# Mask products of windowed attention on two strips of 32 rows, with a fixed mask per tile whose outer strip GpSimd copies

## The reference

```
heads = 16, width of a head = 8, W = 32
for each block of 32 queries: keys are the 96 positions from 32 before the block to 32 behind it
scores = q @ k.T                                  (q = k = v = x, no projection)
valid  = |k_pos - q_pos| <= 32 and 0 <= k_pos < 1024
p      = softmax(where(valid, scores, -1e9))
out    = p @ v
x      = layernorm(x + attention block(x)) ...
```

## Time and profile before

| what | us |
|---|---|
| median of 3 runs | 635.5 |
| lowest and highest run | 632.0, 638.23 |
| the profiled execution | 636.62 |
| its span, first to last instruction | 634.8 |
| mean granted TensorE clock | 0.963 of full speed |

### The profile page before, as it was taken

How to read it: one execution, slowest core, us unless ns; L and a number is a source line. 1 busy time by engine, 2 the same in 40 slices (tenths; PEclk the granted TensorE clock), 3 DMA queues, 4 the chain that set the end, 5 groups by cost and what they waited for, 6 DMA issues and landing times.

```text
span 634.8 us, 42631 instructions
## 1 busy us (share of the span) xinstructions
PE 520.3 (82%) x17985; PEld 442.4 (70%) x17985; DVE 530.2 (84%) x1761; ACT 427.5 (67%) x845; POOL 405.0 (64%) x522
## 2 busy tenths in 40 slices
PE   0279999999998989996656879889888888888886
PEld 0167888888887658775545768778777777777775
DVE  5657888898988387876578879999999999999982
ACT  3336776777776457765144768787788878887882
POOL 8434546555652153644227768888888888888882
PEclk9989999999999999998786989999999999999999
DMA  6875984745427010000003232333233322333231
GB/s 203 260 236 175 273 251 149 240 134 196 142 95 253 18 33 18 22 13 2 10 8 76 46 78 53 81 79 79 58 74 79 83 62 66 79 83 69 59 79 45
DMA packets 45201, 64.39 MB, mean 101 GB/s; under 512 B 5488, under 2 KB 37360, under 8 KB 42608
## 3 DMA queue, kind: packets, MB, share of 16 engines
q1 hardware_dynamic: 45168, 63.97, 36.1%
HBM read 36.29 MB, written 8.65 MB: 71 GB/s over the span
## 4 chain that ended last, share of the span: by engine, by line
PE 38%; DVE 36%; issue 12%; DMA 5%; POOL 4%; SPq 2%; ACT 2%; DVEq 1%; POOLq 0%; ACTq 0%
PE ps L756 7%; DVE top L1398 7%; DVE wq_sb L1429 6%; DVE hid L1446 5%; PE ps L815 5%; DVE prod L1455 5%; PE ps L828 4%; DVE r_x L1440 4%; PE ps L736 4%; PE ps L771 4%; DVE best L1409 3%; PE ps L921 3%; PE ps L746 3%; DMA xT<-terms 2%; PE ps L782 2%
## 5 line engine op out<-in xcount | busy, mean ns | idle before, releaser
L921 PE MATMUL ps<-arena,hid 128*32 128x32 f32 x8192 | 80.0, 200 | 43.2 <-DVE hid L1446 35.8
L921 PEld LDWEIGHTS ps<-arena,hid 128*32 128x32 f32 x8192 | 76.1, 112 | 49.4 <-issue 26.0
L970 ACT ACTIVATE arena<-ps 128x512 f32<-128x512 f32 x128 | 70.0, 595 | 55.4 <-PE ps L756 55.2
L1189 DVE TENSOR_REDUCE row_max<-ps 128x8 f32<-128x768 f32 x64 | 61.0, 953 | 19.7 <-PE ps L746 19.3
L930 PEld LDWEIGHTS ps<-xT,downT_sb 128*128 128x128 f32 x528 | 67.1, 199 | 13.1 <-issue 12.0
L756 PE MATMUL ps<-ident,arena 128*128 128x128 f32 x512 | 70.3, 283 | 0.0
L930 PE MATMUL ps<-xT,downT_sb 128*128 (+1 forms) x528 | 66.9, 282 | 0.0
L942 PE MATMUL ps<-up_sb,prod 128*128 128x128 f32 x512 | 65.6, 282 | 0.3 <-DVE prod L1455 0.3
L670 POOL TENSOR_TENSOR wq_sb<-wq_sb,tile_rows 128x1024 f32<-128x1024 f32 x32 | 65.1, 2036 | 0.7 <-POOL tile_rows L664 0.6
L1192 DVE TENSOR_TENSOR arena<-ps,row_max 128x768 f32<-128x768 f32 x64 | 61.3, 958 | 5.1 <-DVE row_max L1189 0.2
L736 PE MATMUL ps<-tile_rows 100*32 100x96 bf16 x2112 | 36.7, 214 | 34.2 <-POOL tile_rows L561 24.9
(11 more groups left out here) (162 smaller groups left out, 1325.9 us busy)
## 6 DMA issues: line engine op xcount, KB each, us to landing
arena<-r_x SPq DMA_DIRECT2D x128, 128.0 KB, 2.4
early<-terms SPq DMA_DIRECT2D x8, 720.0 KB
xT<-terms SPq DMA_DIRECT2D x8, 720.0 KB
hid<-terms SPq DMA_DIRECT2D x8, 720.0 KB
prod<-terms SPq DMA_DIRECT2D x8, 720.0 KB
x_pair<-in_x_wrapped SPq DMA_DIRECT2D x16, 256.0 KB
xT_tile<-xT SPq DMA_DIRECT2D x34, 64.0 KB, 1.9
x<-in_x SPq DMA_DIRECT2D x8, 256.0 KB, 2.7
```

The costliest lines, as they stand in the source:

```text
L921: mm = nc.tensor.matmul(slots[32 * g:32 * g + 32, k, c], leftT[p][:, r // 2, r % 2, :], blocks_of[p][:, :, r // 2, r % 2, GROUP * g:GROUP ...
L970: return nc.scalar.activation(out_ap, in_ap, ACT.Copy)
L1189: V.tensor_reduce(mx.rearrange("p (a b) -> p a b", a=2), sc, AX_X, ALU.max).then_inc(max_done, 1)
```

## The change

The identity of 128 x 128 is replaced by `lanes`: 64 rows in bf16, each strip of 32 rows being four 32 x 32 identities side by side. The mask is the same in each strip of 32 rows, so 32 rows of `lanes` with 32 rows of the mask give the same 128 rows of output. The first group of a half uses rows 0 to 31, the second rows 32 to 63.

The moving operand has a fixed place now: windows 8 to 11 for the first tile of a pair, 12 to 15 for the second. Only one strip of these is not always the same: the first third of window 8 (the first tile may begin a sequence) and the last third of window 15 (the second tile may end one). `copy_rows` on POOL copies this strip, 64 rows x 32 columns of bf16, from one of the four windows that fit, for each tile, ahead of the two row copies, under the same wait. It counts on `rows_ready`, which thus goes up by three for each tile; the waits of PE and SP are changed to match. The register work for the mask's place moves from PE to POOL. DVE makes `lanes` once at the start, and POOL waits for the mask before its first copy.

```diff
@@ names
         band = sb("band", [W, WIN])
+        lanes = sb("lanes", [2 * W, P], BF16)
         mask = sb("mask", [P, 5 * BLOCKS * WIN], BF16)
@@ SP
-                    sp.wait_ge(rows_ready, 4 * i)
+                    sp.wait_ge(rows_ready, 6 * i)
@@ POOL, copy_rows
                 need(pool, scores_done, GROUPS * (t - 1))
                 hold(pool)
                 at = p * (P // 2)
+                block = (2 * j + u) % 4
+                if p == 0:
+                    end, source = mask[0:2 * W, 8 * WIN:8 * WIN + W], mask[0:2 * W, bass.ds(block * WIN, W)]
+                else:
+                    end, source = mask[0:2 * W, 16 * WIN - W:16 * WIN], mask[0:2 * W, bass.ds((17 + block) * WIN - W, W)]
+                nc.gpsimd.tensor_copy(end, source).then_inc(rows_ready, 1)
                 nc.gpsimd.tensor_copy(q_words[p], q_pairs[u][:, :, at + W // 2:at + W // 2 + P // 2]).then_inc(rows_ready, 1)
                 nc.gpsimd.tensor_copy(k_words[p], k_pairs[u][:, :, at:at + TILE_KEYS // 2]).then_inc(rows_ready, 1)
...
+            pool.wait_ge(mask_ready, 3)
             copy_rows(0, 0, 0)
...
-            pool.sem_inc(rows_ready, 2)
+            pool.sem_inc(rows_ready, 3)
@@ PE
-            pe.wait_ge(mask_ready, 3)
+            pe.wait_ge(mask_ready, 4)
@@ PE, scores
-                mask_at = bass.ds((i % 4 + p) * (BLOCKS * WIN), BLOCKS * WIN)
+                tile_mask = mask[:, (2 + p) * BLOCKS * WIN:(3 + p) * BLOCKS * WIN]
                 if half == 0:
-                    pe.wait_ge(rows_ready, 2 * (t + 1))
+                    pe.wait_ge(rows_ready, 3 * (t + 1))
...
                 for g in groups:
-                    nc.tensor.matmul(edges_of(ps[:, g, 0:BLOCKS * WIN]), ident_bf[:], edges_of(mask[:, mask_at]),
+                    rows = slice(W * (g % 2), W * (g % 2) + W)
+                    nc.tensor.matmul(edges_of(ps[:, g, 0:BLOCKS * WIN]), lanes[rows, :], edges_of(tile_mask[rows]),
                                      start=False, stop=True, skip_group_check=True).then_inc(scores_done, 1)
@@ DVE
+            V.tensor_copy(lanes[:].rearrange("p (q c) -> p q c", q=4), bcast(fold4[0:2 * W], 1, 4)).then_inc(mask_ready, 1)
```

## The result

The changed kernel is slower: 639.34 us in the median of 20 runs beside 635.92 us for the kernel before, a ratio of 1.0055 (95% interval 1.0035 to 1.0075). A second series of the same kernel gave 1.0032 (1.0002 to 1.0063), with medians of 636.88 and 635.76 us. Forecast were 634.6 us and a range up to 638.6. The loss is within the 1% to which "no change" had been given 0.81, but its sign is not the one forecast. The median of the first series lies outside the range, that of the second inside it. The profiled execution took 638.81 us, with a span of 636.9 us.

What follows compares the result with a forecast made beforehand. PE's own stream was taken as the limit from 97 to 193 us, row transfers from 57 to 97. Terms of -0.8, -0.3 and +0.2 gave -0.9 us, from 635.5 to 634.6 us; range 629.8 to 638.6.

Steps and rivals of the forecast that it cites:

- no change: Whole kernel: the total stays within 1% of the kernel before, chance 0.81.
- step 3: Attention: 42 half tiles gain 0.02 us each, 0.8 us; halves between 57 and 97 us count nothing.
- Step 1: Mask products on PE: on disjoint row strips they start together, saving the 0.12 us between their starts.
- Step 2: PE, mask products to transposes: new division change costs 0.09 us, leaving a gain of about 0.02 us per half tile.
- The second rival: End of each mask step: strips do not overlap and the array drains, 3.8 us lost, total 639.5 us; chance 0.11.
- either sign of being wrong: Attention: PE's share from 97 to 193 us under 95%, or POOL's copy over 1 us.
- Steps 5 and 6: POOL's 0.2 us copy hidden except the first, +0.2 us; PE's dropped register instruction and DVE's extra work: nothing.
- step 4: Start, before 57 us: eight halves with PE on the chain gain 0.3 us, 1.6 us at the upper bound.

Runs made afterwards that it cites:

- before_again: The kernel before, unchanged, run once more for a second profile: ratio 1.0 (0.9974 to 1.0026) to the kernel before.
- after_again: The changed kernel, unchanged, run once more for a second profile: ratio 1.0032 (1.0002 to 1.0063) to the kernel before.
- one_strip: The changed kernel with both mask products of a half tile on rows 0 to 31: 644.45 us, ratio 1.0133 to the kernel before.
- the strips alone: The changed kernel without POOL's strip copy and its count, two sequence ends left unmasked: ratio 1.002 (1.0003 to 1.0037) to the kernel before.

## Why the prediction was wrong

**What bounds the kernel: right from 97 us on, open between 57 and 97 us.** From 97 us on PE's stream is the limit, before and after. For the stretch ahead of it step 3 said that the transfers absorb what PE gains or loses. The times fit: from the first mask product of the tile at 56 us to that at 99 us it is 42.68 us before and 42.48 after (tiles at 55.08 and 97.56), and 41.91 and 42.28 in the second profiles. The means are 0.1 us apart, where PE alone would make it 0.7 (0.09 us for each of eight tiles). But the two profiles of the kernel before are 0.77 us apart. And the chain of the kernel after still runs through a transfer there (80.59, 11.26 us) and comes back through v_mid, at 94.77 us, while in `before_again` and `after_again` the chain from 55 to 98 us has no transfer and runs over matmuls for 96% and 85% of the time. One profile of the chain was too little to leave this stretch out of the sum.

**Step 1, overlap of row strips, taken as true: right,** shown by `one_strip`.

**Step 2, a drain of 0.09 us at the new change of division: right to 0.01 us.** Forecast 0.20 to 0.21 us from first mask product to first transpose, measured 0.21. The gain there is 0.017 us, not 0.02.

**Where it failed: step 2 stopped at the start of the first transpose.** The sum counted the time up to that start as if all behind it stayed as it was. It priced the drain as a gap between two products, and put at nothing, without a reason, the weight load of the first product behind it, whose cover a drain takes away. For each half tile that term is +0.056 us, and it turned -0.02 into +0.04. With it, step 3 reads 42 x 0.039 = +1.6 us. The timelines say the same over nine tiles: before, from the mask product at 150.61 to that at 197.26 it is 46.65 us; after, from 150.11 to 197.59, it is 47.48: 0.09 us for each tile, 1.9 us over the 21 tiles of the 42 halves. The count of 42 is right, but no records of mask products are missing: the 76 are 38 halves, and four more follow. The profile of before held what was needed: the load of the first transpose started with the second mask product and 0.11 us ahead of its own. A warning sign stood in the numbers used, too: the second mask product, 0.12 us behind the first and not 0.107.

**The second rival had the sign and nearly the size, by another mechanism.** It put +3.8 us on strips that do not overlap. They do. Its own test, "the distance is above 0.23 us", says no, and yet the kernel is slower; the test looked only as far as the first transpose. Nor did either sign of being wrong show: PE's share from 97 to 193 us is 97%, and POOL's copy takes 0.2 us. Of the signs named, only the pair of tiles gives the mistake away: 10.51 us, where 10.25 to 10.29 was forecast.

**Steps 5 and 6, POOL's copy: right in the steady part.** It takes 0.204 us (forecast 0.2) and its runs hide in POOL's idle time in the steady part (1.90 us ahead of it at 152.42, up to 2.4 elsewhere). In the chain stands the first, as said, and between 57 and 97 us one more in each profile (0.12 us at 92.22, 0.20 us at 77.54 in the second). The register instruction taken off PE gave nothing, as said.

**What stays open.** The steady part accounts for 1.7 to 1.9 us. The measured ratios put the loss at 3.5 and 2.0 us, with intervals that overlap between 0.35% and 0.63%, or 2.2 to 4.0 us. Up to 0.7 us more can come from the stretch from 57 to 97 us, if PE sets the pace there. The end of attention adds 0.2 us at most at the same clock; whether the clock falls more often there with the change, two profiles of each kernel can't tell. The start of the kernel after is even ahead in both of its profiles, so that by the mask product at 197 us they stand at 197.59 and 196.33 us, beside 197.26 and 197.46 before: the loss of the total can't be followed there. The 0.3 us of step 4 for the start can't be told from this either. The interval of the strips alone (0.03 to 0.37% in the first series) holds the 1.7 us.

## What to carry to other kernels

Price a change of the array's division from both sides: the drain (here 0.09 to 0.10 us behind the streaming of the last product), and the weight load of the first product behind it, which nothing covers any more. A wait on TensorE exposes that load as well. Two products on side-by-side strips did not pay here: their saving, 0.11 us, is below both costs together, 0.15 us. A chain of waits from one profile can differ in the next of the same kernel, so a stretch is left out of a sum only with more than one. And where the expected effect is a few tenths of a per cent, read it from a steady stretch between two fixed instructions, which here repeated to 0.01 us, and not from the total, which wavered by 1%.

## What the runs showed of the hardware

- Mask products on rows 0 to 31 and 32 to 63, each with 128 columns out and each into its own PSUM bank, start 3 to 4 ns apart: two at once write 128 partitions each, and the transpose behind them comes 0.11 us earlier than behind two on the same rows (0.212 and 0.318 us behind the first).
- The drain between divisions was 0.09 to 0.10 us in all four kinds seen: whole array to column strips, column strips to whole array, column strips to row strips (0.138 us from the start of the last score product, in both kernels, with 0.04 for its 96 columns at full clock), and row strips of 32 or 64 to the whole array. The Trainium skill (TensorEngine Tiling (Array Packing), Key Properties) says "Mode switching requires drain"; the trace agrees, now for rows as well.
- A load of 128 columns of fp32 weights that nothing covers cost 0.056 us, behind a drain and behind a wait alike. One of bf16, behind a drain, cost 0.013.
- From 193 to 222 us the granted clock was 0.88, 0.94 or 1.00 from one profile to the next, of the same kernel too, and the end of attention took 21.6 to 21.9, 20.6 or 19.1 us (all profiles but that of `one_strip`).
- At a fixed clock the engine's stream repeats to 0.01 us in 90, from run to run and between kernels whose instructions on TensorE are the same.
